# Attention loop over batches written out, row sums inverted on GpSimd instead of VectorE

## The chip, the core and the metric

The kernel runs on one core of a Trainium2 chip. The metric is the time of one execution on the device, in microseconds (us). Engines are named as the profile names them: PE is TensorE (matmuls; PEld its weight loads), DVE is VectorE, ACT is ScalarE, POOL is GpSimd, SP is SyncE, which here issues the DMAs.

## The reference

One transformer block with adaptive layer norm, in float32, on x of shape (4, 512, 128): 4 batches of 512 tokens, width 128. The attention half has 16 heads of width 64 and a relative position bias; the second half is a mixture of 160 experts, top 8 for each token.

```python
mod = (silu(c) @ wmod)                       # shift, scale, gate for both halves
h = layernorm(x) * (1 + ca) + sa
q, k, v = split(h @ qkv_w.T)                 # 16 heads of 64
scores = einsum("bhqd,bhkd->bhqk", q, k) * 64 ** -0.5 + bias
attn = softmax(scores, axis=-1)              # rows of 512
a = einsum("bhqk,bhkd->bhqd", attn, v)
x = x + ga * (a @ o_w.T)
h = layernorm(x) * (1 + cb) + sb
x = x + gb * moe(h)                          # 160 experts, top 8
```

The change touches the softmax (the division by the row sum) and the order of the work around it.

## The kernel before

Each engine has its own instruction stream, written by hand; the streams meet only at semaphores (`wait_ge`, `then_inc`). An engine executes its stream in order, so an instruction that waits holds up everything behind it on that engine.

The attention half takes the batches one after the other. Within a batch the 16 heads go in 8 pairs (`HPAIRS`), `pair(b, n)`. A pair has 8 units (`UNITS`): 2 heads times 4 tiles of 128 query rows. A unit `u` is a 128x512 tile of scores (128 query rows, 512 keys) and passes through these steps:

- PE, `scores` (L409, L411): two matmuls into PSUM bank `BANK_S + g % 2`, so two units at a time.
- DVE, `add_bias` (L976): adds the bias, writes the tile into `prob[:, u, :]` and its negated row maximum into `nmax`. It waits until the tile of the same `u` of the pair before has been transposed.
- ACT, `exponential` (L706): exp in place, with the row sum into `rsum[:, u]`; it counts `s_exp`.
- DVE, `invert_sums` (L993): after every second unit, one reciprocal of the two columns `rsum[:, u:u+2]` into `rinv`; it counts `s_rinv`.
- POOL, `normalise` (L859): multiplies the 128x512 tile by its column of `rinv`; it counts `s_prob`.
- PE, `transpose_probs` (L420): four 128x128 transposes into PSUM; DVE (odd units) or ACT (even units) copies them to `PT` (L204).
- PE, `attend` (L433): 16 matmuls for each pair, `PT` by `v_sb`, into `BANK_O`; DVE, `copy_o` (L999), copies the result to `oT`; PE, `project_out` (L446), adds it to y in `BANK_Y`.

Besides these, every pair projects Q and K of the pair two ahead (`project_qk`, L383; `qk_high` on ACT, `qk_low` on DVE, L959) and V of the next ones (`project_v`, L394), and SP restacks Q and K by DMA (`stack_pair`).

The order is software pipelined by hand: `pair(b, n)` on PE issues scores of pair n, two units at a time, and between them the transposes and `attend` of pairs n, n-1 and n-2. Pairs 8 and 9 of a batch are pairs 0 and 1 of the next one. Pairs (0, 0) and (0, 1) stand alone in the code. Then comes a hardware loop of 3 iterations over the batch, `Fori(0, B - 1)`, with the 8 pairs n = 2 to 9 in its body, on SP, PE, ACT and DVE, and behind it the 6 last pairs of batch 3, written out. POOL has a loop of its own, `Fori(0, B)`, with 64 units in the body. Semaphore counts that depend on the batch are compared with a register inside the loops.

At the end of a batch, in pair n = 9 (`HPAIRS + 1`), DVE gates y (`gate_y`, L1004), PE transposes it (`transpose_y`, L453), and DVE adds it to x (`update_x`, L1019) and takes the statistics of the new x for the second layer norm (`new_statistics`, L1011, four tiles). These two DVE steps are the last ones of the loop's body:

```python
                if n == HPAIRS + 1:
                    update_x(b)
                    new_statistics(b)
```

What waits for `update_x` is `project_out` of the next batch's first pair, issued in its pair 2, since it writes the same PSUM bank. `project_out` waits for `copy_o` too. The expert half after the attention has loops of its own, which the change leaves alone.

Of the kernel before, what the change touches and what calls it, by code (L numbers as in the profile page):

```python
# [24 lines left out]
P = 128  # L25
B, S, D = 4, 512, 128
# [8 lines left out]
HPAIRS = H // 2  # L35
UNITS = 2 * QT
# [19 lines left out]
def adaln_block(nc, x, emb, qkv_t, o_t, router_t, expert_bias, gate_t_in, down_t, gate_shared_t,  # L56
# [4 lines left out]
    G = HPAIRS * UNITS  # L61
# [7 lines left out]
    with ctx:  # L69
        def sb(name, shape, dt=F32):  # L70
            return ctx.enter_context(nc.sbuf_tensor(name, shape, dt))

        def sem(name):
            return ctx.enter_context(nc.semaphore(name))
# [25 lines left out]
        nmax = sb("nmax", [P, UNITS])  # L100
        rsum = sb("rsum", [P, UNITS])
        rinv = sb("rinv", [P, UNITS])
        modT = sb("modT", [P, 6, B])
        gate_t = sb("gate_t", [P, 2, B])
        cT = sb("cT", [P, B])
# [59 lines left out]
        s_s, s_ttr, s_exp, s_t = sem("scores"), sem("biased"), sem("exped"), sem("transposed")  # L165
        s_ca, s_cd = sem("copied_by_act"), sem("copied_by_dve")
        s_v, s_vc, s_pv = sem("v_projected"), sem("v_copied"), sem("pv_done")
        s_rinv, s_prob, s_o = sem("sums_inverted"), sem("normalised"), sem("o_copied")
        s_ymm, s_yg, s_ytr, s_x2 = sem("y_added"), sem("y_gated"), sem("y_transposed"), sem("x_updated")

# [45 lines left out]
        apart = sem("apart")  # L216
# [5 lines left out]
        def _(sp):  # L222
# [32 lines left out]
            def stack_pair(b, n):  # L255

                par = n % 2
                if n >= 2:
                    sp.wait_ge(s_s, b * G + UNITS * (n - 1))
                    sp.sem_inc(apart, 1)  # L260
                projected = b * HPAIRS + (n + 1)
                halves = ((0, slice(0, HD), slice(HD, P)), (1, slice(HD, P), slice(0, HD)))
                sp.wait_ge(s_qkh, projected)
                sp.sem_inc(apart, 1)
                for head, own, _ in halves:
                    sp.dma_start(stack[own, par, head, :, :].bitcast(F32),
                                 qkH[own, :, :].bitcast(F32)).then_inc(s_stack[par], 16)
                sp.wait_ge(s_qkl, projected)
                sp.sem_inc(apart, 1)
                for head, own, other in halves:  # L270
                    sp.dma_start(stack[other, par, head, :, :].bitcast(F32),
                                 qk[own, 0:4:3, :].bitcast(F32)).then_inc(s_stack[par], 16)
                    sp.dma_start(kLow[par][own, head, :].bitcast(F32),
                                 qkL[own, 1, :].bitcast(F32)).then_inc(s_stack[par], 16)
                    sp.dma_start(kLow[par][other, head, :].bitcast(F32),
                                 qkL[own, 1, :].bitcast(F32)).then_inc(s_stack[par], 16)
# [12 lines left out]
            sp.dma_start(wdsT[:, :], down_shared_t).then_inc(ld["small"], 16)  # L289
            sp.dma_start(ebias[:, 0:1], expert_bias[0:P, :]).then_inc(ld["small"], 16)  # L290
            sp.dma_start(ebias[0:E - P, 1:2], expert_bias[P:E, :]).then_inc(ld["small"], 16)
            with sp.Fori(0, B - 1) as b:
                for n in range(2, HPAIRS + 2):
                    if n == HPAIRS - 2:
                        sp.wait_ge(s_v, b * HPAIRS + HPAIRS)
                        sp.sem_inc(apart, 1)
                        sp.dma_start(hcur[:, :, :].bitcast(F32), hT[:, bass.ds(b + 1, 1), :, :].rearrange(
                            "p o l s -> p (o l) s").bitcast(F32)).then_inc(ld["hcur"], 16)
                    stack_pair(b, n + 2)
# [48 lines left out]
        def _(pe):  # L348
# [157 lines left out]
            pair(0, 1)  # L506
            pe.wait_ge(w_split, 6)
            pe.wait_ge(ld["ow"], 16)
            with pe.Fori(0, B - 1) as b:
                for n in range(2, HPAIRS + 2):  # L510
                    pair(b, n)
            for n in range(2, HPAIRS):
# [157 lines left out]
        def _(act):  # L670
# [87 lines left out]
            first_high(1)  # L758
            pair(0, 0)
            pair(0, 1)  # L760
            with act.Fori(0, B - 1) as b:
                for n in range(2, HPAIRS + 2):
                    pair(b, n)
            for n in range(2, HPAIRS):
# [87 lines left out]
        @block.gpsimd  # L852
        def _(pool):
            def normalise(b, n, u):

                if u % 2 == 0:
                    pool.wait_ge(s_rinv, b * (G // 2) + (UNITS * n + u) // 2 + 1)
                    pool.sem_inc(apart, 1)
                nc.gpsimd.tensor_scalar(prob[:, u, :], prob[:, u, :], rinv[:, u:u + 1], None,  # L859
                                        ALU.mult).then_inc(s_prob, 1)  # L860

            with pool.Fori(0, B) as b:
                for n in range(HPAIRS):
                    for u in range(UNITS):
                        normalise(b, n, u)
# [3 lines left out]
        def _(dve):  # L869
# [51 lines left out]
            def first_low(n):  # L921
                b = FIRST_ORDER[n]
                modulated_low(n, hcur if b == 0 else hT[:, b, :, :], h_full[b])
# [33 lines left out]
            def qk_low(b, n):  # L957
                dve.wait_ge(s_qkh, b * HPAIRS + (n + 1))
                nc.vector.tensor_tensor(qkL[:, :, :], ps[:, BANK_PROJ:BANK_PROJ + 2, :],  # L959
                                        qkH[:, :, :].bitcast(F32), ALU.subtract).then_inc(s_qkl, 1)  # L960
# [23 lines left out]
                    dve.wait_ge(s_pv, b * HPAIRS + (n - 1))  # L984
                copy_unit(nc.vector.tensor_copy, n, u).then_inc(s_cd, 1)

            def invert_sums(b, n, u):

                g = UNITS * n + u
                dve.wait_ge(s_exp, b * G + (g + 2))  # L990
                if n >= 1:
                    dve.wait_ge(s_prob, b * G + (g - UNITS + 2))
                nc.vector.reciprocal(rinv[:, u:u + 2], rsum[:, u:u + 2]).then_inc(s_rinv, 1)  # L993

            def copy_o(b, n):
                dve.wait_ge(s_pv, b * HPAIRS + (n + 1))
                if n >= 2:
                    dve.wait_ge(s_ymm, b * HPAIRS + (n - 1))
                nc.vector.tensor_copy(oT[:, n % 2, :], ps[:, BANK_O, :]).then_inc(s_o, 1)  # L999
# [7 lines left out]
            def new_statistics(b):  # L1007

                dve.wait_ge(s_x2, b + (1 + X2_AHEAD))
                for t in range(QT):  # L1010
                    last = nc.vector.bn_stats(  # L1011
                        stats[:, bass.ds(b * QT + t, 1), :].rearrange("p o k -> p (o k)"),
                        x_all[:, bass.ds(b, 1), t * D:(t + 1) * D].rearrange("p o d -> p (o d)"))
                last.then_inc(s_stats, 1)

            def update_x(b):
                dve.wait_ge(s_ytr, b + 1)
                x_b = x_all[:, bass.ds(b, 1), :].rearrange("p o n -> p (o n)")
                nc.vector.tensor_tensor(x_b, x_b, ps[:, BANK_Y, :], ALU.add).then_inc(s_x2, 1)  # L1019

            def pair(b, n, final=False):

                add_bias(b, n, 0)
                add_bias(b, n, 1)
                if n == 0:
                    first_low(1)
                    qk_low(b, 1)
                if n >= 2:
                    copy_o(b, n - 2)
                if n >= 1:  # L1030
                    copy_probs(b, n - 1, 5)
                invert_sums(b, n, 0)

                add_bias(b, n, 2)
                add_bias(b, n, 3)
                if n == 0:
                    modulate(2)
                    modulate(3)
                if n >= 1:
                    copy_probs(b, n - 1, 7)  # L1040
                invert_sums(b, n, 2)

                add_bias(b, n, 4)
                add_bias(b, n, 5)
                if n == HPAIRS + 1:
                    gate_y(b)
                if n == 0:
                    qkv_low(3)
                    qkv_low(4)
                    qkv_low(5)  # L1050
                copy_probs(b, n, 1)
                invert_sums(b, n, 4)

                add_bias(b, n, 6)
                add_bias(b, n, 7)
                if n == 0:
                    first_low(2)
                    first_low(3)
                copy_probs(b, n, 3)
                invert_sums(b, n, 6)  # L1060
                if not (final and n >= HPAIRS - 2):
                    qk_low(b, n + 2)
                if n == HPAIRS + 1:
                    update_x(b)
                    new_statistics(b)

            qk_low(0, 0)
            then(statistics(3))
# [2 lines left out]
            for b in range(1, B):  # L1071
                norm(b, xn)
            modulate(1)
            pair(0, 0)
            pair(0, 1)
            sign_gates()
            with dve.Fori(0, B - 1) as b:
                for n in range(2, HPAIRS + 2):
                    pair(b, n)
            for n in range(2, HPAIRS):  # L1080
# [157 lines left out]
```

## Time and profile before

| | |
|---|---|
| median of 3 runs | 1015.85 us (1013.87 to 1016.39) |
| profiled execution, its own time | 1013.81 us |
| span of the profile | 1012.0 us |
| granted TensorE clock, mean | 0.985 of full speed |
| busy in the span | PE 94%, DVE 76%, ACT 67%, POOL 39% |
| attention half | about 25 to 517 us of the span |
| expert half | the rest |

The span runs from the first to the last instruction of the core; the 1.8 us between span and time lie around it. Busy time is counted for each engine over the whole span, so POOL, which works in the attention half alone, is far busier there than its 39% say. "Idle before" in a row is the time that the engine did nothing just before an instruction, with what released it behind the arrow.

### The profile page before, as it was taken

What the parts mean: (1) busy time and instruction counts of PE and PEld (TensorE: products, weight loads), DVE (VectorE), ACT (ScalarE), POOL (GpSimd) and SP (SyncE); (2) the same over time, 40 slices, a digit from 0 to 9 for tenths busy, and PEclk for the clock granted to TensorE, in tenths of its full rate; (3) what the DMA queues carried; (4) which work ended last, traced back from release to release, by engine and by line L of the source; (5) the groups of instructions that cost most, each with busy time, mean ns of one, the idle gap of its engine ahead of it and who ended that gap; (6) DMA issues with size and microseconds to landing.
All of it is one profiled execution on the core that took longest, in us unless ns stands there. A gap on an engine that the chain in (4) does not pass through costs nothing.

```text
span 1012.0 us, 16804 instructions
## 1 busy us (share of the span) xinstructions
PE 953.2 (94%) x4592; PEld 690.6 (68%) x4592; DVE 769.4 (76%) x1452; ACT 679.4 (67%) x1168; POOL 398.1 (39%) x260
## 2 busy tenths in 40 slices
PE   4889999899998999999969699999999999999997
PEld 2546666566665666666524578888888888888886
DVE  5757667566665666766647589999999999999997
ACT  3556666466665666666626477877777777777775
POOL 0578888688886888888910000000000000000000
PEclk9999999899999999999979899999999999999999
DMA  7885445256444445534200899999999999999991
GB/s 205 258 234 119 97 119 126 63 124 142 113 96 101 96 118 125 125 90 99 66 19 27 204 221 219 223 222 222 223 222 222 221 224 221 223 220 225 220 206 41
DMA packets 71096, 160.39 MB, mean 158 GB/s; under 512 B 10273, under 2 KB 36193, under 8 KB 60945
## 3 DMA queue, kind: packets, MB, share of 16 engines
q1 hardware_dynamic: 71056, 159.97, 70.1%
q8 instruction: 13, 0.21, 0.1%
q14 instruction: 27, 0.21, 0.1%
HBM read 105.60 MB, written 2.42 MB: 107 GB/s over the span
## 4 chain that ended last, share of the span: by engine, by line
PE 84%; DMA 4%; DVE 4%; issue 3%; ACT 2%; SPq 1%; POOL 1%; POOLq 0%; DVEq 0%; ACTq 0%
PE ps L620 40%; PE ps L433 11%; PE ps L420 10%; PE ps L409 5%; PE ps L411 5%; PE ps L383 4%; PE ps L446 3%; PE ps L394 2%; DMA strips<-in_L_ffn_w_down 2%; DMA k_low<-qk 1%; POOL prob L859 1%; DMA comb_rows<-strips 1%; PE ps L538 1%; PE ps L540 0%; DVE qk L959 0%
## 5 line engine op out<-in xcount | busy, mean ns | idle before, releaser
L859 POOL TENSOR_SCALAR prob<-prob,rinv 128x512 f32<-128x512 f32 x256 | 397.9, 1567 | 111.3 <-DVE rinv L993 109.1
L706 ACT ACTIVATE prob<-prob,nmax 128x512 f32<-128x512 f32 x256 | 182.9, 716 | 150.9 <-DVE nmax L976 150.8
L620 PE MATMUL ps<-hT,wT 128*128 128x512 f32 x960 | 244.2, 390 | 0.3 <-DVE wT L1145 0.3
L1164 DVE TENSOR_TENSOR PT<-v_sb,strips 128x1024 f32<-128x1024 f32 x160 | 196.0, 1225 | 41.4 <-ACT v_sb L830 28.3
L830 ACT ACTIVATE v_sb<-ps 128x1024 f32<-128x1024 f32 x160 | 164.5, 1028 | 77.9 <-PE ps L620 77.4
L620 PEld LDWEIGHTS ps<-hT,wT 128*128 128x128 f32 x960 | 180.8, 189 | 39.0 <-ACT strips L805 1.1
L620 PE MATMUL ps<-stack,wT 128*128 128x512 f32 x640 | 198.1, 391 | 9.2 <-DVE wT L1151 9.2
L204 DVE COPY PT<-ps 128x512 f32<-128x512 f32 x128 | 88.4, 691 | 141.2 <-PE ps L420 138.7
L1151 DVE TENSOR_TENSOR wT<-PT,stack 128x1024 fp32r<-128x1024 f32 x160 | 195.0, 1219 | 0.0
L976 DVE CUSTOM_DVE_ANT_0 prob<-ps,strips 128x512 f32<-128x512 f32 x256 | 165.0, 681 | 11.5 <-issue 8.0
L822 ACT CAST stack<-PT 128x1024 fp32r<-128x1024 f32 x160 | 166.6, 1041 | 8.8 <-DVE PT L1164 8.8
L420 PEld LDWEIGHTS ps<-ident,prob 128*128 128x128 f32 x1024 | 114.7, 141 | 76.8 <-issue 39.1
L620 PEld LDWEIGHTS ps<-stack,wT 128*128 128x128 f32 x640 | 120.3, 189 | 35.7 <-DVE wT L1151 10.9
L420 PE MATMUL ps<-ident,prob 128*128 128x128 f32 x1024 | 137.5, 277 | 2.9 <-ACT PT L204 1.4
L409 PE MATMUL ps<-stack 128*128 128x512 f32 x256 | 114.3, 447 | 15.7 <-DVE nmax L976 9.9
L433 PE MATMUL ps<-PT,v_sb 128*64 128x512 f32 x512 | 124.5, 608 | 2.6 <-ACT PT L204 1.4
L620 PE MATMUL ps<-wT 128*128 128x512 f32 x320 | 99.0, 391 | 0.0
L204 ACT COPY PT<-ps 128x512 f32<-128x512 f32 x128 | 73.9, 578 | 20.8 <-PE ps L420 20.8
L433 PEld LDWEIGHTS ps<-PT,v_sb 128*64 128x64 f32 x512 | 31.8, 137 | 63.1 <-issue 50.8
L620 PEld LDWEIGHTS ps<-wT 128*128 128x128 f32 x320 | 60.4, 189 | 12.6
L409 PEld LDWEIGHTS ps<-stack 128*128 128x128 f32 x256 | 49.4, 193 | 23.9 <-DVE nmax L976 11.8
L383 PE MATMUL ps<-hcur,wT 128*128 128x512 f32 x192 | 52.2, 409 | 3.5 <-DVE hcur L918 3.5
(105 smaller groups left out, 731.1 us busy)
## 6 DMA issues: line engine op xcount, KB each, us to landing
strips<-comb_rows SPq DMA_DIRECT2D x158, 512.0 KB, 10.9
stack<-qk SPq DMA_DIRECT2D x128, 256.0 KB, 3.8
k_low<-qk SPq DMA_DIRECT2D x64, 128.0 KB, 3.9
hT<-qk SPq DMA_DIRECT2D x64, 128.0 KB, 3.8
strips<-bias_rows SPq DMA_DIRECT2D x3, 1792.0 KB, 13.9
strips<-in_L_ffn_w_gate SPq DMA_DIRECT2D x80, 64.0 KB, 9.8
strips<-in_L_ffn_w_down SPq DMA_DIRECT2D x80, 64.0 KB, 11.0
strips<-bias_rows SPq DMA_DIRECT2D x2, 896.0 KB, 5.4
```

The lines of the kernel that those rows point to most:

```text
L204: return copy(dst[:, :, qt * P:(qt + 1) * P], ps[:, BANK_T + u % 2, :].rearrange("p (k s) -> p k s", s=P))
L409: nc.tensor.matmul(ps[:, BANK_S + g % 2, :], stack[:, par, head, 0, qt * P:(qt + 1) * P], stack[:, par, head, 1, :], start=True, stop=False)
L420: last = nc.tensor.transpose(ps[:, BANK_T + u % 2, kb * P:(kb + 1) * P], prob[:, u, kb * P:(kb + 1) * P], ident[:, :])
L433: last = nc.tensor.matmul(ps[head * HD:(head + 1) * HD, BANK_O, :], v_sb[:, (n // 2) % 2, kb, (n % 2) * P + head * HD:(n % 2) * P + (head ...
L620: last = nc.tensor.matmul(ps[:, bank + c, :], weights(a), rows(m, c), start=start and k == 0, stop=stop and k == 2, skip_group_check=True)
L706: nc.scalar.activation(prob[:, u, :], prob[:, u, :], ACT.Exp, bias=nmax[:, u:u + 1], scale=-1.0, accum_out=rsum[:, u:u + 1]).then_inc(s_ex ...
L822: nc.scalar.copy(h_high[:, k % 4, :], weighted[:, k % 4, :]).then_inc(s_hh, 1)
L830: nc.scalar.activation(silu[:, k % 2, :], ps[:, BANK_G + 2 * half:BANK_G + 2 * half + 2, :].rearrange("p c s -> p (c s)"), ACT.Silu).then_ ...
L859: nc.gpsimd.tensor_scalar(prob[:, u, :], prob[:, u, :], rinv[:, u:u + 1], None, ALU.mult).then_inc(s_prob, 1)
L976: nc.vector.tensor_tensor_reduce(out=prob[:, u, :], in0=ps[:, BANK_S + u % 2, :], in1=backwards, scale=-1.0, scalar=3.0e38, op0=ALU.add, o ...
L1151: nc.vector.tensor_tensor(h_low[:, k % 4, :], weighted[:, k % 4, :], h_high[:, k % 4, :].bitcast(F32), ALU.subtract).then_inc(s_hl, 1)
L1164: nc.vector.tensor_tensor(weighted[:, k % 4, :], silu[:, k % 2, :], cb[:, r, half * HALF:(half + 1) * HALF], ALU.mult).then_inc(s_mul, 1)
```

## The change

1. The loops over the batch are ordinary Python loops, on SP, PE, ACT, DVE and POOL: their 3 (POOL: 4) iterations are written out as straight code, with constant semaphore counts.
2. `invert_sums` is gone from DVE. POOL does it in `normalise`, with a `tensor_tensor` power of -1 on the same two columns (the exponents in a new 128x2 tile `minus_one`, filled once), and waits for its own result before the multiplication.
3. `update_x` and `new_statistics` of a batch move on DVE from the end of its pair 9 to the next pair (pair 2 of the next batch), behind `add_bias` of units 0 and 1 and ahead of `copy_o`.

```diff
+        minus_one = sb("minus_one", [P, 2])
...
+        s_exponents = sem("exponents_set")
...
-            with sp.Fori(0, B - 1) as b:
+            for b in range(B - 1):
                 for n in range(2, HPAIRS + 2):
...
-            with pe.Fori(0, B - 1) as b:
+            for b in range(B - 1):
...
-            with act.Fori(0, B - 1) as b:
+            for b in range(B - 1):
...
+                g = UNITS * n + u
                 if u % 2 == 0:
-                    pool.wait_ge(s_rinv, b * (G // 2) + (UNITS * n + u) // 2 + 1)
-                    pool.sem_inc(apart, 1)
+                    pool.wait_ge(s_exp, b * G + (g + 2))
+                    nc.gpsimd.tensor_tensor(rinv[:, u:u + 2], rsum[:, u:u + 2], minus_one[:, :], ALU.pow).then_inc(s_rinv, 1)
+                    pool.wait_ge(s_rinv, b * (G // 2) + g // 2 + 1)
                 nc.gpsimd.tensor_scalar(prob[:, u, :], prob[:, u, :], rinv[:, u:u + 1], None,
                                         ALU.mult).then_inc(s_prob, 1)
...
-            with pool.Fori(0, B) as b:
+            nc.gpsimd.memset(minus_one[:, :], -1.0).then_inc(s_exponents, 1)
+            pool.wait_ge(s_exponents, 1)
+            for b in range(B):
...
-            def invert_sums(b, n, u):
-
-                g = UNITS * n + u
-                dve.wait_ge(s_exp, b * G + (g + 2))
-                if n >= 1:
-                    dve.wait_ge(s_prob, b * G + (g - UNITS + 2))
-                nc.vector.reciprocal(rinv[:, u:u + 2], rsum[:, u:u + 2]).then_inc(s_rinv, 1)
...
                 if n == 0:
                     first_low(1)
                     qk_low(b, 1)
+                if n == 2 and b >= 1:
+                    update_x(b - 1)
+                    new_statistics(b - 1)
                 if n >= 2:
                     copy_o(b, n - 2)
                 if n >= 1:
                     copy_probs(b, n - 1, 5)
-                invert_sums(b, n, 0)
...
-                if n == HPAIRS + 1:
-                    update_x(b)
-                    new_statistics(b)
...
-            with dve.Fori(0, B - 1) as b:
+            for b in range(B - 1):
                 for n in range(2, HPAIRS + 2):
                     pair(b, n)
```

The other three calls of `invert_sums` in `pair` (units 2, 4 and 6) go as well.

## Rows read from the trace of the kernel before

**Rows 1.** The page, busy shares and POOL's line over 40 equal slices.

```profile
PE 953.2 (94%) x4592; PEld 690.6 (68%) x4592; DVE 769.4 (76%) x1452; ACT 679.4 (67%) x1168; POOL 398.1 (39%) x260
...
POOL 0578888688886888888910000000000000000000
```

**Rows 2.** Busy time by stretch: us, PE, PEld, DVE, ACT, POOL, PEclk, DMA, GB/s.

```profile
180.00:202.00 22.00, 17.36 (x82) 11.19 (x83) 11.80 (x32) 9.57 (x22) 12.77 (x9) 0.84 0.31 73
201.50:301.00 99.50, 99.50 (x551) 65.78 (x550) 68.02 (x184) 66.71 (x155) 86.99 (x57) 1.00 0.50 116
...
437.46:508.00 70.54, 70.52 (x387) 44.54 (x386) 48.57 (x131) 45.87 (x109) 63.46 (x42) 1.00 0.42 96
```

**Rows 3.** Waits from 208.7 to 293.7 us: total us, times, longest.

```profile
POOL prob L859 <- DVE rinv L993: 10.0, 18, 0.8
```

**Rows 4.** The chain that ended last: start us, us, what; some of the attends, transpose of y, one wait.

```profile
158.29 1.87 PE ps L433 x8
...
172.49 1.87 PE ps L433 x8
...
176.32 0.44 PE ps L453 x4
...
182.56 3.65 issue
...
194.50 1.94 PE ps L433 x8
...
293.73 1.87 PE ps L433 x8
...
314.88 1.94 PE ps L433 x8
...
414.35 1.87 PE ps L433 x8
...
430.40 1.94 PE ps L433 x8
...
444.64 1.87 PE ps L433 x8
```

**Rows 5.** Timeline where the loop jumps back: start us, us, what, [idle before].

```profile
180.85 0.68 DVE L1019 TENSOR_TENSOR x_all<-x_all,ps 128x512 f32 x1
...
181.70 1.00 DVE L1011 BATCH_NORM_STATS2 stats<-x_all  x4 [0.17 <-DVE x_all L1019]
...
186.57 0.69 DVE L976 CUSTOM_DVE_ANT_0 prob<-ps,strips 128x512 f32<-128x512 f32 x1 [3.87 <-issue]
...
187.32 0.80 PE L409 MATMUL ps<-stack 128*128 128x512 f32 x1 [4.50 <-DVE nmax L976]
```

**Rows 6.** Timeline of an undisturbed pair, units 0 and 1.

```profile
260.37 0.69 DVE L999 COPY oT<-ps 128x512 f32<-128x512 f32 x1
...
261.21 0.19 ACT L706 ACTIVATION_READ_ACCUMULATOR prob<-prob,nmax 128x1 f32 x1
...
261.76 0.16 DVE L993 RECIPROCAL rinv<-rsum 128x2 f32<-128x2 f32 x1
...
262.12 3.10 POOL L859 TENSOR_SCALAR prob<-prob,rinv 128x512 f32<-128x512 f32 x2 [0.70 <-DVE rinv L993]
...
262.58 1.02 PE L446 MATMUL ps<-oT,woT 128*128 128x512 f32 x2
```

**Rows 7.** Groups and lines: durations (mean ns, or min/median/max) on POOL and DVE.

```profile
L859 POOL TENSOR_SCALAR prob<-prob,rinv 128x512 f32<-128x512 f32 x256 | 397.9, 1567 | 111.3 <-DVE rinv L993 109.1
L1226 POOL MEMSET const-float32-0.0<- 128x1 f32 x1 | 0.1, 99 | 0.2 <-issue 0.2
...
L993 DVE RECIPROCAL rinv<-rsum x128: 148/155/167, 36.3 to 505.3; 128x2 f32<-128x2 f32 x128
...
L976 DVE CUSTOM_DVE_ANT_0 prob<-ps,strips 128x512 f32<-128x512 f32 x256 | 165.0, 681 | 11.5 <-issue 8.0
```

**Rows 8.** Timeline, POOL at the end of the attention half.

```profile
491.12 18.51 POOL L859 TENSOR_SCALAR prob<-prob,rinv 128x512 f32<-128x512 f32 x12 [0.71 <-DVE rinv L993]
```

More of the change, by code:

```diff
@@ L1040, in pair @@
                     copy_probs(b, n - 1, 7)
-                invert_sums(b, n, 2)
                 add_bias(b, n, 4)
@@ L1051, in pair @@
                 copy_probs(b, n, 1)
-                invert_sums(b, n, 4)
                 add_bias(b, n, 6)
@@ L1059, in pair @@
                 copy_probs(b, n, 3)
-                invert_sums(b, n, 6)
                 if not (final and n >= HPAIRS - 2):
                     qk_low(b, n + 2)
-                if n == HPAIRS + 1:
-                    update_x(b)
-                    new_statistics(b)
             qk_low(0, 0)
```

## The prediction

> **What bounds the kernel now.** I began with the page. PE is busy for 94% of the span; POOL's 39% is an average over a half where it works and one where it has nothing to do, and in the slices of the attention half it stands at 8 tenths [rows 1]. So two engines matter for the change: PE, which probably sets the pace, and POOL, to which work is added. The busy time by stretch shows that first guess to be right: from 201.5 to 301 us PE is busy for 99.50 of 99.50 us, POOL for 86.99, or 87%, and DVE for 68% [rows 2]. In an undisturbed stretch nothing but PE's own work sets the time; a faster DVE or POOL gains nothing there.
>
> The chain that ended last gives the beat. An `attend` block comes back every pair: 172.49 - 158.29 = 14.20 us [rows 4]. POOL's share of a pair is 8 tiles. It ran 12 of them in 18.51 us where it never waited, and 3.10 us is a usual time for two [rows 6, 8], so 1.56 us each and 12.5 us a pair; 14.20 - 12.5 = 1.7 us are free. The waits agree: over 85 us, six pairs, POOL waited 10.0 us for the reciprocals, 1.67 us a pair [rows 3].
>
> Then I looked for where PE doesn't keep this beat. The same block around the batch boundaries, each step holding one pair: 194.50 - 172.49 = 22.01, 314.88 - 293.73 = 21.15, and 430.40 - 414.35 = 16.05 us [rows 4]. Against 14.20 these are 7.8, 6.95 and 1.85 us too much, 16.6 us in all. The first two boundaries are those where the loop jumps back, the third falls out of the loop. The timeline says what the jump does: DVE has finished the statistics at 182.7 us and then stands for 3.87 us waiting for nothing but its own next instruction, PE idles 4.50 us for the bias tile that comes after it [rows 5], and the granted clock of that stretch falls to 0.84, between the levels of 2.4 and 1.2 GHz, after that idle time [rows 2].
>
> **The change, part by part.**
>
> *Loops written out.* The two jumps go. What shows their price is the third boundary, which has the same work and no jump: 7.8 + 6.95 - 2 x 1.85 = 11.05 us. Straight code does not run slower: the last batch is written out already and keeps its pair in 444.64 - 430.40 = 14.24 us [rows 4], with PE busy for 70.52 of 70.54 us [rows 2]. The jumps of PE, ACT, SP and POOL lie under DVE's, and they go too. Gain 11.05 us; the bounds are 0 (if fetching the code stalls elsewhere) and 15 (the whole excess of both).
>
> The Trainium skill, Runtime: NRT & Kernel Launch, section Instruction fetch mechanics, says that a jump out of the small window of loaded code costs a fetch, while straight code is prefetched. That explains the 3.65 us of "issue" [rows 4], and by it too the jumps would be the whole price.
>
> *`update_x` and `new_statistics` moved.* At the third boundary they hold DVE for 0.68 + 0.17 + 1.00 us [rows 5] in front of `add_bias`, and PE pays 1.85 us. Of these, 0.44 us is PE's own transposing of y [rows 4], which stays. In the new place two tiles of bias go first and PE can go on with the scores; late is now `copy_o`. In an undisturbed pair it starts at 260.37 and ends at 261.06, and `project_out`, which needs it, starts at 262.58 [rows 6]: 1.52 us of cover against 1.85 + 0.1 us of delay, so PE waits about 0.5 us. New price of a boundary: 0.44 + 0.5, say 0.95 us instead of 1.85, for three boundaries a gain of 2.7 us. Bounds: 0, and 4.2 if the delay is hidden altogether. If POOL has no slack left, the same delay (the exponentials of units 2 and 3 come 1.9 us later) falls on it as well.
>
> *Reciprocal off DVE.* 128 reciprocals of 155 ns [rows 7], 0.6 us a pair, on an engine that is not the bound: nothing by itself. What hides them is PE's full beat. Without them POOL no longer waits behind DVE's queue: the row sum of unit 1 is out at 261.40, the reciprocal begins at 261.76 and POOL starts 0.70 us after its last tile [rows 6]. That wait is room for the new work, and it is the 1.7 us a pair counted above.
>
> *The power on POOL.* Four a pair, 128 in all; each costs POOL its duration d and a wait s for its own result, since the multiplication behind it cannot be handed over before. For s a row is near: DVE waits 0.17 us between an instruction and its dependent one [rows 5]. For d there is none: the trace has no power and no small two-input instruction on POOL. From below: a POOL memset of 128x1 takes 0.10 us [rows 7]. From above: if the whole duration of a 128x512 multiplication were fixed, 1.56 us. Between them, DVE does the same 128x2 shape in 0.155 us, and POOL is 1567/681 = 2.3 times as slow as DVE on a 128x512 tile [rows 7]: 0.36 us. The power itself is unknown work on only 2 columns. I take the middle of 0.10 and 0.36, d = 0.23, as the operation is nearest to these small rows, and so d + s = 0.40 us. Four make 1.6 us, and POOL has 1.7 us. So it just fits: undisturbed pairs keep 14.20 us. The whole argument hangs here, and the room left is 0.02 us in each power. Where it doesn't fit, POOL sets the beat and each 0.01 us above 0.42 costs 4 x 0.01 x 30 pairs = 1.2 us.
>
> The Trainium skill, GPSIMD Engine Reference, section Performance versus the Vector engine, speaks against this part: ordinary elementwise work is about 1.96 times slower there. By an estimate from that page and DVE's 155 ns, d would be 0.30 and the sum further down would read -5 instead of -12 us; no run here shows a two-input instruction on POOL.
>
> *The end of the attention half.* In the last two pairs PE has less to do, and POOL runs its last 12 tiles without a pause from 491.12 us [rows 8]; what follows waits for its last tile. There the powers are not hidden: six of them at 0.40, of which the first begins 0.7 us earlier than the tile did. That is 6 x 0.40 - 0.7 = +1.7 us. At the start, POOL's first tiles also follow each other closely, but PE then waits for a DMA, which hides it.
>
> *Sum.* -11.05 - 2.7 + 1.7 = -12.05 us against the profiled execution's own 1013.81: 1001.8 us. That execution was 2.0 us below the median of the runs; I put half of that on top for a median: **1002.7 us**.
>
> **Rivals.**
>
> - *POOL becomes the bound.* This one ends on the other side. For it: 87% busy already, and four dependent small instructions more a pair. Against: their size, if the small rows are a guide. With x = d + s the change is -13.75 + (6x - 0.7) + 120 (x - 0.42) us. It is zero at x = 0.515, that is d = 0.345 us: from there on the gain is eaten. At d = 0.6 (x = 0.77) the sum is 31.6 us, 1045 us; at the upper bound d = 1.56 it is +154 us, 1168 us. Chance 0.26 for d above 0.35 by enough to be seen.
> - *It fits only partly*: x between 0.42 and 0.515, and the time between 1002 and 1014 us. For it: the ratio row gives just the upper end. Chance 0.17, most of it still faster than the bound below.
> - *Writing out brings nothing*: the stall at the batch boundary is not the jump but code that has to be loaded, and the far longer streams stall somewhere else. Against it speaks the third boundary, without a stall, and the last batch. Time: 1013.8 - 2.7 + 1.7 = 1012.8 us. Chance 0.07.
>
> **How the numbers follow.** The forecast itself (x up to 0.42) has 0.50. A measurement of this kernel can tell about 0.3%, 3 us, from no change. Faster: 0.50 + 0.13 from the partial case + 0.02 from the third rival = 0.65. Same: 0.03 + 0.05 = 0.08. Slower: 0.26 + 0.01 = 0.27. Both signs hold a good part, so the range is wide: its low end, 996 us, is the sum with all three boundaries free of excess (-16.6 and a little off the end), its high end, 1045 us, is POOL as the bound with d = 0.6; beyond it I leave 0.14, below it 0.04. The likeliest case alone lies between 998 and 1006 us.
>
> **What the profile after should show.** The 3.65 us of "issue" on the chain and the 4.50 us idle of PE are gone at both boundaries, and the granted clock stays at 1.00 there. The `attend` steps over the three boundaries are about 15.1 us. A new POOL row, 128 powers of 128x2, some 0.2 us each, followed by about 0.17 us of waiting for itself. POOL is busy for over 90% of an undisturbed pair, which still takes 14.2 us with PE fully busy. If instead the `attend` steps are all longer than 14.2 and PE waits for POOL's `prob`, the size of the power was wrong, and the excess of a pair divided by four tells by how much. What would make the prediction wrong is that one number, far more than all others.

## The result, and the profile after

| | median | runs | ratio to before, 95% interval |
|---|---|---|---|
| before | 1014.89 us | 1013.87 to 1016.39 | |
| after | 1043.38 us | 1042.78 to 1044.88 | 1.0282 [1.0262, 1.0301] |

The changed kernel is 28.5 us, 2.8%, slower. The forecast was 1002.7 us, faster: the sign was wrong. The time lies at the upper edge of the range, where the first rival stood, with 0.26: POOL becomes the bound. The kernel before ran again beside each group of experiments, and every ratio is to those runs: their medians were 1014.89 us here, 1014.66 us beside e1 to e4, and 1015.95 us beside e5 to e8.

The page of the changed kernel: busy shares, PE's and POOL's line over the slices, the chain by engine and by line, and the two POOL groups.

```profile
PE 966.4 (93%) x4592; PEld 684.4 (66%) x4592; DVE 764.3 (73%) x1324; ACT 679.8 (65%) x1168; POOL 487.9 (47%) x389
...
PE   4789999999999999999977699999999999999997
...
POOL 0689999999999999999960000000000000000000
...
PE 44%; POOL 44%; DMA 4%; DVE 2%; issue 2%; SPq 2%; ACT 1%; POOLq 0%; ACTq 0%; DVEq 0%
PE ps L622 39%; POOL prob L863 36%; POOL rinv L861 8%; DMA strips<-in_L_ffn_w_down 2%; DMA k_low<-qk 2%; SPq L315 1%; DMA comb_rows<-strips 1%; PE ps L540 1%; PE ps L385 0%; PE ps L435 0%; PE ps L542 0%; PE ps L555 0%; ACT qk L704 0%; PE ps L593 0%; PE ps L355 0%
...
L863 POOL TENSOR_SCALAR prob<-prob,rinv 128x512 f32<-128x512 f32 x256 | 399.8, 1573 | 12.6
...
L861 POOL TENSOR_TENSOR rinv<-rsum,minus_one 128x2 f32<-128x2 f32 x128 | 92.0, 719 | 35.8 <-ACT prob L708 35.8
```

POOL stands at 9 tenths where it stood at 8 [rows 1]. On the chain it has 44% of the span, all of it in the attention half, where the chain ran over PE before. The power is a row of 128 instructions of 719 ns. POOL's idle time is 35.8 us, nearly all before its first power, against 111.3 us before [rows 7].

Busy time in 77.9 us, five pairs of POOL's new beat (columns as in [rows 2]), and POOL's timeline there:

```profile
208.30:286.20 77.90, 73.87 (x391) 46.37 (x390) 47.58 (x111) 47.33 (x111) 75.93 (x61) 1.00 0.46 109
```

```profile
201.84 0.72 POOL L861 TENSOR_TENSOR rinv<-rsum,minus_one 128x2 f32<-128x2 f32 x1
202.66 3.11 POOL L863 TENSOR_SCALAR prob<-prob,rinv 128x512 f32<-128x512 f32 x2
205.73 0.72 POOL L861 TENSOR_TENSOR rinv<-rsum,minus_one 128x2 f32<-128x2 f32 x1
206.55 3.11 POOL L863 TENSOR_SCALAR prob<-prob,rinv 128x512 f32<-128x512 f32 x2
```

Two tiles start every 206.55 - 202.66 = 3.89 us: 3.11 of tiles, 0.68 of power (it takes 0.72 but begins 0.04 before the tile ahead has ended) and 0.10 until the tile behind it starts. Four of these are 15.58 us a pair (so one is 3.895 us, more exactly), where PE set 14.20 before. PE is now the one that waits, busy for 73.87 of 77.90 us (before, 99.50 of 99.50 [rows 2]).

The boundary of the batches, where 7.8 us were lost before, from PE's timeline:

```profile
172.28 1.94 PE L435 MATMUL ps<-PT,v_sb 128*64 128x512 f32 x8
...
178.56 0.66 PE L422 MATMUL ps<-ident,prob 128*128 128x128 f32 x4 [0.32 <-POOL prob L863]
...
187.87 1.51 PE L435 MATMUL ps<-PT,v_sb 128*64 128x512 f32 x6
```

The step is 187.87 - 172.28 = 15.59 us, the 15.58 us of any pair, so the stall of the jump is gone. Nothing else of the boundary is left in the step either: whatever PE or DVE loses there hides behind POOL.

### The profile page after: what moved, and what is told of

Same layout as the page of the kernel before. It is cut to its first block, busy times and chain, and to the rows that moved or that the text cites. A ratio compares the mean times of both kernels' runs of the same rounds, so it can differ in the third digit from the quotient of the medians.

```text
span 1041.4 us, 15577 instructions
## 1 busy us (share of the span) xinstructions
PE 966.4 (93%) x4592; PEld 684.4 (66%) x4592; DVE 764.3 (73%) x1324; ACT 679.8 (65%) x1168; POOL 487.9 (47%) x389
## 4 chain that ended last, share of the span: by engine, by line
PE 44%; POOL 44%; DMA 4%; DVE 2%; issue 2%; SPq 2%; ACT 1%; POOLq 0%; ACTq 0%; DVEq 0%
PE ps L622 39%; POOL prob L863 36%; POOL rinv L861 8%; DMA strips<-in_L_ffn_w_down 2%; DMA k_low<-qk 2%; SPq L315 1%; DMA comb_rows<-strips 1%; PE ps L540 1%; PE ps L385 0%; PE ps L435 0%; PE ps L542 0%; PE ps L555 0%; ACT qk L704 0%; PE ps L593 0%; PE ps L355 0%
## 5 line engine op out<-in xcount | busy, mean ns | idle before, releaser
L422 PEld LDWEIGHTS ps<-ident,prob 128*128 128x128 f32 x1024 | 112.5, 141 | 121.9 <-issue 57.3
L422 PE MATMUL ps<-ident,prob 128*128 128x128 f32 x1024 | 154.3, 283 | 28.9 <-POOL prob L863 28.2
L435 PE MATMUL ps<-PT,v_sb 128*64 128x512 f32 x512 | 127.4, 620 | 1.9 <-ACT PT L206 1.1
L861 POOL TENSOR_TENSOR rinv<-rsum,minus_one 128x2 f32<-128x2 f32 x128 | 92.0, 719 | 35.8 <-ACT prob L708 35.8
```

The source lines that it names most:

```text
L422: last = nc.tensor.transpose(ps[:, BANK_T + u % 2, kb * P:(kb + 1) * P], prob[:, u, kb * P:(kb + 1) * P], ident[:, :])
L861: nc.gpsimd.tensor_tensor(rinv[:, u:u + 2], rsum[:, u:u + 2], minus_one[:, :], ALU.pow).then_inc(s_rinv, 1)
```

## The experiments

The theory after the result: the power costs POOL 0.72 us and not 0.23; POOL sets the beat; the rest of the change is a gain. Eight kernels test this against its rivals.

### e1 and e2: without the power

e1 is the kernel before with the loops written out; the `sem_inc` behind each POOL wait, which stood only in the loop, goes with them. e2 is the changed kernel with `invert_sums` back on DVE, so it differs from e1 by the moved update of x:

```diff
-            with dve.Fori(0, B - 1) as b:
+            for b in range(B - 1):
```

That was e1 against before, on all five engines alike. e2 against after, where the call on DVE stands for units 2, 4 and 6 too:

```diff
-                    nc.gpsimd.tensor_tensor(rinv[:, u:u + 2], rsum[:, u:u + 2], minus_one[:, :], ALU.pow).then_inc(s_rinv, 1)
...
+                invert_sums(b, n, 0)
```

Expected of e1:

> The kernel before with the batch loops written out on all engines and nothing else. Theory A (the power's 0.72 us on POOL is the whole loss, writing out is a gain of its own): the jumps' price goes, 1014.9 - 11 = about 1004 us, the two PE waits of 4.5 us are gone and DVE's 3.87 us of issue too. Theory B (the long straight streams themselves are loaded more slowly, and that is part of the loss): 1015 us or above, with stalls named issue or by engine queues spread over the attention half.

Expected of e2:

> The changed kernel with the reciprocals back on DVE: loops written out and the update of x moved, no power on POOL. Theory A: 1004 - 2.7 = about 1001 us, with some 15.1 us for the attend steps across the three boundaries. Rival: the move only shifts the delay from the bias tiles to the copy of o and gains nothing, then it equals the written-out kernel, about 1004 us. Theory B: no better than 1015 us.

Measured: e1 1001.67 us, ratio 0.9870 [0.9854, 0.9887]; e2 1000.33 us, 0.9865 [0.9849, 0.9881]. Writing out is a gain, and a rival in which straight code stalls falls with it. DVE's idle time named issue before its bias tiles is 0.2 us in all in e1, against 8.0 us before [rows 7], and the granted clock at the first boundary (180 to 195 us) is 1.00, where it was 0.84 [rows 2]. The chain of e1 across two boundaries:

```profile
172.45 1.87 PE ps L435 x8
188.03 1.94 PE ps L435 x8
...
287.27 1.87 PE ps L435 x8
302.85 1.94 PE ps L435 x8
```

The steps are 15.58 us, the third one (417.66 - 402.08) as well, against 22.01, 21.15 and 16.05 before [rows 4]: 12.5 us less in sum, against a gain of 13.0 us measured. It is more than the 11.05 expected, since the third boundary, which had no stall, became 0.47 us shorter too, and each of the others by as much again. DVE's timeline at the third boundary before, and at the first one in e1:

```profile
422.71 0.68 DVE L1019 TENSOR_TENSOR x_all<-x_all,ps 128x512 f32 x1
...
424.65 0.69 DVE L976 CUSTOM_DVE_ANT_0 prob<-ps,strips 128x512 f32<-128x512 f32 x1
```

```profile
180.81 0.67 DVE L1020 TENSOR_TENSOR x_all<-x_all,ps 128x512 f32<-128x512 f32 x1
...
181.52 0.87 DVE L1012 BATCH_NORM_STATS2 stats<-x_all 128x6 f32<-128x128 f32 x4
...
182.31 0.67 DVE L977 CUSTOM_DVE_ANT_0 prob<-ps,strips 128x512 f32<-128x512 f32 x1
```

From the update of x to the next bias tile DVE takes 1.94 us in the loop and 1.50 us in straight code (the same at its other two boundaries): it waits 0.04 us for its own result instead of 0.17, and the four statistics take 0.87 us instead of 1.00 [rows 5].

In e2 the step is still 15.58 us, not the 15.1 expected: the move gained nothing at the boundary, as the rival had it. That e2's time nevertheless came out at theory A's 1001 us is luck. The profiled executions of e1 and e2 differ by 3.0 us already at 172.45 and 169.49 us, the last `attend` on the chain ahead of the first boundary, up to which the move changes nothing, and the intervals of the two ratios overlap. e2's timeline there:

```profile
179.06 0.68 DVE L1020 TENSOR_TENSOR x_all<-x_all,ps 128x512 f32<-128x512 f32 x1
...
179.78 0.88 DVE L1012 BATCH_NORM_STATS2 stats<-x_all 128x6 f32<-128x128 f32 x4
...
180.57 0.68 DVE L1000 COPY oT<-ps 128x512 f32<-128x512 f32 x1
...
181.30 1.13 PE L448 MATMUL ps<-oT,woT 128*128 128x512 f32 x2
...
181.83 0.67 DVE L977 CUSTOM_DVE_ANT_0 prob<-ps,strips 128x512 f32<-128x512 f32 x1
...
182.54 0.72 ACT L708 ACTIVATE prob<-prob,nmax 128x512 f32<-128x512 f32 x1 [1.98 <-DVE nmax L977]
...
184.44 0.58 ACT L206 COPY PT<-ps 128x512 f32<-128x512 f32 x1
...
185.07 1.51 PE L435 MATMUL ps<-PT,v_sb 128*64 128x512 f32 x6 [0.85 <-ACT PT L206]
```

`project_out` (L448) starts in its turn, 0.05 us after `copy_o` (L1000) ends, so the cover over `copy_o` held better than forecast. What is late is the bias of units 2 and 3 (L977), then ACT, which waits 1.98 us for it, and then ACT's copy to `PT`, queued behind two exponentials and the copy of V: `attend` waits 0.85 us for it.

### e3: the power alone

The kernel before with loops and order kept, and the power on POOL in place of `invert_sums`:

```diff
                 if u % 2 == 0:
-                    pool.wait_ge(s_rinv, b * (G // 2) + (UNITS * n + u) // 2 + 1)
+                    pool.wait_ge(s_exp, b * G + (g + 2))
                     pool.sem_inc(apart, 1)
+                    nc.gpsimd.tensor_tensor(rinv[:, u:u + 2], rsum[:, u:u + 2], minus_one[:, :], ALU.pow).then_inc(s_rinv, 1)
+                    pool.wait_ge(s_rinv, b * (G // 2) + g // 2 + 1)
+                    pool.sem_inc(apart, 1)
```

> The kernel before, loops kept and update of x in its old place, with the reciprocals replaced by the power on POOL. Theory A (POOL sets the beat of 3.9 us for two units, 15.6 us a pair): slower than the changed kernel's 1043.4, since the jumps still stop DVE and POOL runs dry there: POOL idled 6.2 us at each jump before, of which its work ahead hides part, so 1047 to 1054 us. Theory B (half of the loss is from the straight code): below 1035 us.

Measured: 1062.42 us, 1.0471 [1.0453, 1.0488]. The direction is theory A's, the size is above its 1047 to 1054. So on top of the power, the written-out loops and the move together are worth 19.0 us (e3 against after), more than the 14.5 us without it (e2 against before). POOL's timeline says why:

```profile
185.27 3.11 POOL L865 TENSOR_SCALAR prob<-prob,rinv 128x512 f32<-128x512 f32 x2 [0.21 <-POOL rinv L862]
...
189.28 3.11 POOL L865 TENSOR_SCALAR prob<-prob,rinv 128x512 f32<-128x512 f32 x2 [0.21 <-POOL rinv L862]
...
199.16 0.72 POOL L862 TENSOR_TENSOR rinv<-rsum,minus_one 128x2 f32<-128x2 f32 x1 [2.77 <-ACT prob L708]
```

At the jump POOL runs dry for 2.77 us, and for 2.74 us at the second one: 5.5 us. And its beat is 4.01 us instead of 3.89, since it stands 0.21 us between the power and the tile, against 0.10 in the changed kernel: 128 x 0.11 = 14 us, which the expectation did not have. Together 19.5 us. e3 also has the update of x in its old place. POOL does not wait at the third boundary, which has that update and no jump, so the update alone does not run it dry; what share it has in the 5.5 us, no run tells. In the loop the wait is against a register and followed by a semaphore increment; which of the two costs the 0.11 us, no run tells apart.

### e4: a list of prices on POOL

e2 with scratch instructions, each waiting for the one before, in POOL's idle time at the start:

```python
            nc.gpsimd.tensor_tensor(pc[:, 0:2], pa[:, 0:2], pb[:, 0:2], ALU.pow).then_inc(s_pa, 1)
            pool.wait_ge(s_pa, 3)
            ...
```

> The kernel of e2 with extra instructions at the head of POOL's stream, where it has 36 us to spare, on scratch tiles: powers of 2, 4, 16 and 64 columns, two-input products of 2 and 64 columns, a one-input product of 2 and 256 columns, a copy of 2 columns, each twice. Theory fixed (every small two-input instruction on POOL costs about 0.7 us): the product of 2 columns takes about 0.7 us as the power does, and 4 columns cost no more than 2. Theory per element (the power is computed column by column at a high price): the product of 2 columns takes 0.1 to 0.2 us, and the power grows by about 0.3 us a column, so 1.3 us for 4 and 5 us for 16. The whole time may be some us above e2 if the list takes longer than the spare time.

Measured: 1001.37 us (one run), and the timeline of POOL's first 36 us; L869 to L883 are powers, L885 to L891 products of two tiles, L893 and L901 products with a column of scalars. The list ended at 36.8 us, and POOL's first tile started 3.2 us later than in e2 (36.86 against 33.67 us); the time lies within e2's range all the same (999.17 to 1002.34 us).

```profile
1.21 0.72 POOL L869 TENSOR_TENSOR pc<-pa,pb 128x2 f32<-128x2 f32 x1
2.01 0.70 POOL L871 TENSOR_TENSOR pc<-pa,pb 128x2 f32<-128x2 f32 x1
...
2.79 1.01 POOL L873 TENSOR_TENSOR pc<-pa,pb 128x4 f32<-128x4 f32 x1
...
4.96 2.90 POOL L877 TENSOR_TENSOR pc<-pa,pb 128x16 f32<-128x16 f32 x1
...
10.91 10.54 POOL L881 TENSOR_TENSOR pc<-pa,pb 128x64 f32<-128x64 f32 x1
...
32.16 0.19 POOL L885 TENSOR_TENSOR pc<-pa,pb 128x2 f32<-128x2 f32 x1
...
32.71 0.32 POOL L889 TENSOR_TENSOR pc<-pa,pb 128x64 f32<-128x64 f32 x1
...
33.53 0.30 POOL L893 TENSOR_SCALAR pc<-pa 128x2 f32<-128x2 f32 x1
...
34.81 0.93 POOL L901 TENSOR_SCALAR pc<-pa 128x256 f32<-128x256 f32 x1
```

A power costs (10.54 - 2.90)/48 = 0.16 us a column, as it does from 4 to 16 columns, and some 0.4 us that don't depend on the width. A product of the same shape costs 0.19 us, and 0.002 us a column. Neither theory is right alone: of the 0.72 us, about 0.2 us is what the product of the same shape costs, 0.3 us are the two columns, and the other 0.2 us is a fixed part of the power. The price by the column is there, but half of the 0.3 us expected. The second power is as dear as the first (0.70 us), so no cost of a first use shows.

### e5, e6 and e7: the beat, moved from three sides

All three are the changed kernel with one thing else. e5 puts a product in place of the power. e6 keeps the power and makes the tiles narrower. e7 puts a product in its place that is nearly as long as the power. The waits stay. What they leave out is a right result: e5 scales the rows by a wrong factor, e6 leaves the last 96 columns of each tile unscaled, e7 scales every tile by a constant. In this order, e5, e6 and e7:

```diff
-                    nc.gpsimd.tensor_tensor(rinv[:, u:u + 2], rsum[:, u:u + 2], minus_one[:, :], ALU.pow).then_inc(s_rinv, 1)
+                    nc.gpsimd.tensor_tensor(rinv[:, u:u + 2], rsum[:, u:u + 2], minus_one[:, :], ALU.mult).then_inc(s_rinv, 1)
```

```diff
-                nc.gpsimd.tensor_scalar(prob[:, u, :], prob[:, u, :], rinv[:, u:u + 1], None,
+                nc.gpsimd.tensor_scalar(prob[:, u, 0:416], prob[:, u, 0:416], rinv[:, u:u + 1], None,
```

```diff
-                    nc.gpsimd.tensor_tensor(rinv[:, u:u + 2], rsum[:, u:u + 2], minus_one[:, :], ALU.pow).then_inc(s_rinv, 1)
+                    nc.gpsimd.tensor_tensor(pc[:, :], pa[:, :], pb[:, :], ALU.mult).then_inc(s_rinv, 1)
```

> The changed kernel with the power replaced by a two-input product on the same 128x2 tiles, so the rows are scaled by the wrong factor; all waits stay. The list of prices gave 0.195 us for it against 0.70 to 0.72. Theory size (only d matters, POOL has 0.42 us for each power and its wait): 0.195 + 0.10 fits, POOL needs 13.6 us a pair, PE sets the beat of 14.2 again, and the time is that of e2, 1000 to 1002 us. Rival (the dependent wait and the wait for the exponential on POOL itself cost it the beat, whatever the operation): well above 1010 us, with POOL idle before the products.

> The changed kernel with the power kept, but POOL normalises only 416 of the 512 columns of each tile; the other 96 stay unnormalised. Theory size: 96 columns are 0.24 us by the list of prices (2.5 ns a column), 1.9 us a pair, so POOL needs 15.58 - 1.9 = 13.7 us a pair, less than PE's 14.2, and the whole loss goes though all 128 powers are there: 1000 to 1003 us. Rival (the power's latency in the chain from the exponential to the transpose is what PE pays): it stays above 1030 us.

> The changed kernel with the power replaced by a two-input product of 128x176 scratch columns, whose result nothing uses; the tiles are scaled by a constant. By the list of prices it takes 0.195 + 174 x 0.0021 = 0.56 us, and with the wait 0.66 us. Theory size: the time falls by 128 for each us less than the power's 0.785: 1043.4 - 128 x 0.125 = about 1027 us, 15.1 us a pair. Rival (a threshold or anything special to the power, such as its code being loaded each time): e5's time, about 1001 us, since it is a plain product too.

| | two tiles every | POOL a pair | time | ratio, 95% interval |
|---|---|---|---|---|
| after | 3.89 us | 15.58 us | 1043.38 us | 1.0282 [1.0262, 1.0301] |
| e7, product of 176 columns | 3.73 us | 14.9 us | 1022.6 us | 1.0062 [1.0037, 1.0087] |
| e6, tiles of 416 columns | at least 3.42 us | 13.7 us | 1003.19 us | 0.9874 [0.9835, 0.9914] |
| e5, product of 2 columns | at least 3.36 us | 13.4 us | 1002.94 us | 0.9870 [0.9832, 0.9908] |
| e2, no inversion on POOL | PE's beat | 12.5 us | 1000.33 us | 0.9865 [0.9849, 0.9881] |

The second column is from start to start of tiles on POOL's timeline, where POOL does not wait; e7's is half of two beats. Rows of that kind, of e5, e6 and e7:

```profile
202.32 3.10 POOL L863 TENSOR_SCALAR prob<-prob,rinv 128x512 f32<-128x512 f32 x2
...
205.68 3.11 POOL L863 TENSOR_SCALAR prob<-prob,rinv 128x512 f32<-128x512 f32 x2
...
212.83 0.20 POOL L861 TENSOR_TENSOR rinv<-rsum,minus_one 128x2 f32<-128x2 f32 x1 [0.67 <-ACT prob L708]
```

```profile
202.05 2.64 POOL L863 TENSOR_SCALAR prob<-prob,rinv 128x416 f32<-128x416 f32 x2
...
205.47 2.64 POOL L863 TENSOR_SCALAR prob<-prob,rinv 128x416 f32<-128x416 f32 x2
```

```profile
203.60 3.10 POOL L865 TENSOR_SCALAR prob<-prob,rinv 128x512 f32<-128x512 f32 x2
...
211.06 3.10 POOL L865 TENSOR_SCALAR prob<-prob,rinv 128x512 f32<-128x512 f32 x2
```

Busy time in the same 77.9 us, of e5:

```profile
208.30:286.20 77.90, 77.90 (x432) 51.28 (x431) 53.51 (x122) 52.32 (x124) 71.70 (x67) 1.00 0.53 124
```

and of e6 and e7:

```profile
208.30:286.20 77.90, 77.90 (x431) 51.28 (x431) 53.38 (x123) 52.35 (x123) 73.08 (x66) 1.00 0.54 126
```

```profile
208.30:286.20 77.90, 76.17 (x408) 48.99 (x407) 49.18 (x115) 50.06 (x116) 75.84 (x64) 1.00 0.45 109
```

With the product PE is busy all the time again and POOL waits for ACT, though every wait of the new order is there: the duration sets the loss, not the waits. e6 has all 128 powers at full price and PE is busy all the time too: it is not the power's latency in the chain of a unit. e7 is a plain product, and slower than the kernel before: the loss belongs to the length and not to the power. From e7 to the changed kernel the beat grows by 3.895 - 3.73 = 0.165 us, 128 times that is 21 us, and the time grows by 20.8 us (22 us by the ratios). The same slope reaches e2's 1000 us at 3.56 us, about a quarter of PE's 14.20. So a pair takes as long as the slower of the two engines needs for it.

Three misses are small. e5 and e6 lie 1 us or less above the time expected, and some 2.7 us above e2's, with intervals that overlap; of this, 0.7 and 1.2 us are a longer end of the attention half (from one and the same `attend` to the last one 495.64 - 443.39 = 52.25 us in e2, 499.45 - 446.50 = 52.95 in e5, 498.65 - 445.23 = 53.42 in e6). e7 came out 4 us below its 1027: its beat was 0.62 us above the tiles' 3.11, where the expectation had added 0.56 and 0.10 without their overlap of 0.04.

### e8: the statistics later

e2 with `new_statistics` behind the bias of units 2 and 3, where DVE waits for PE anyway:

```diff
                 if n == 2 and b >= 1:
                     update_x(b - 1)
-                    new_statistics(b - 1)
...
+                if n == 2 and b >= 1:
+                    new_statistics(b - 1)
                 if n >= 1:
                     copy_probs(b, n - 1, 7)
```

> e2 with the statistics of the new x taken out of their place behind update_x and put behind the bias of units 2 and 3, where DVE waits for PE; update_x stays where the change puts it. In e2 the step across a boundary is still 15.58 us, as with the loops written out alone: the bias of units 2 and 3 comes 1.5 us late, ACT exponentiates them late, and its copies behind them reach the attend 0.85 us late. Theory: with 0.9 us less on DVE in front, that wait is gone, the steps are 14.7 to 14.8 us and the time 2.4 us below e2's, about 998 us. Rival: what is left is PE's own work and the clock, then the steps stay 15.58 us and the time about 1000 us.

Measured: 999.57 us, 0.9842 [0.9812, 0.9872]. The chain across the first boundary and the second:

```profile
171.52 1.87 PE ps L435 x8
...
186.21 1.94 PE ps L435 x8
...
285.68 1.87 PE ps L435 x8
...
300.36 1.94 PE ps L435 x8
```

The steps are 14.69 and 14.68 us, 0.9 us shorter than e2's at each of three boundaries; what is left over 14.20 is about PE's 0.44 us of transposing y. The chain shows the 2.7 us. The median is only 0.8 us below e2's and above the 998 us expected, and the intervals overlap, so the timed runs do not separate e8 from e2; e8's profiled execution was 2.0 us behind e2's before the first boundary. This kernel has the lowest median here, 1.6% under the kernel before.

## Why the prediction was wrong, by its steps

- *What bounds the kernel*: right. PE's beat of 14.20 us and POOL's 1.7 us of room a pair came out nearly as read. e5, e6 and e7 show the threshold: up to 3.42 us for two tiles PE stays busy all the time, at 3.73 us it does not. A quarter of 14.20 less the 3.11 us of two tiles leaves 0.44 us for a power and its wait, where the prediction had 0.42 (18.51 us for 12 tiles are 1.54 us each, not the 1.56 it went on with).
- *Loops written out*, 11.05 us expected: 12.5 us by the steps, 13.0 us by the time (e1). Right for the stall, a little small: DVE's update of x also runs some 0.4 us shorter outside the loop, at all three boundaries. The Trainium skill, Runtime: NRT & Kernel Launch, section Instruction fetch mechanics, has straight code prefetched and a far jump fetched; the trace agrees: DVE stood 3.87 us at the jump, and in e1 0.2 us in all before the same tiles.
- *Update of x moved*, 2.7 us expected: nothing at the boundary (e2 against e1). Here the mechanism was wrong. I followed the delay to `copy_o` and `project_out`, whose cover held, and did not follow it through the bias of units 2 and 3 to ACT's queue. Moving the statistics behind that bias brings the gain, 0.9 us a boundary (e8).
- *Reciprocal off DVE*: worth nothing by itself, as forecast; e5, without it, is no faster than e2.
- *The end of the attention half*: right as a formula. 6x - 0.7 gives 0.8 us for e5's x of 3.36 - 3.11 = 0.25 us, and 0.7 us was measured.
- *The power on POOL* is the step that failed, and by its size only: d = 0.23 us was forecast from the middle of 0.10 and 0.36 us, and 0.72 us measured. With its wait the forecast had 0.40 us, just inside the room of 0.42; it was 0.785, so POOL's pair took 15.58 us instead of fitting into 14.20, and the sign turned. The error was in the choice of rows. The memset and the multiplication are other operations, and the reciprocal ran on another engine; none of the rows is of a power on POOL. My 0.23 would have been nearly right for the product of the same shape, 0.19 us (e4). I kept the 1.56 us of a full tile as the upper bound but gave the room above 0.35 us only 0.26, though nothing in the trace spoke for it being empty. By the Trainium skill's ratio for elementwise work (GPSIMD Engine Reference, section Performance versus the Vector engine), 1.96, d would by estimate have been 0.30 us; it is a ratio for an addition, and the power measured 0.72 us, the product 0.19 us (e4).
- *The wait for its own result*, 0.17 us: 0.10 measured, 0.21 in a loop (e3). The row that it was taken from stood in a loop as well; DVE's own wait there shrank to 0.04 us in straight code (e1).
- *The rival's formula*, with the measured x = 3.895 - 3.11 = 0.785 us, gives -13.75 + 4.0 + 43.8 = +34 us, measured +28.5. The 120 (x - 0.42) should have been 30 x (15.58 - 14.20) = 41.4, and the 2.9 us that it left standing at the boundaries hide behind POOL; with both mended it gives +28.8 us. The formula was also worked out slightly wrong where its examples stand: d = 0.6 gives +32.2 us and not 31.6, the upper bound +153 and not +154, and d = 0.30 a sum of -5.6 and not -5. The high end of the range, 1045 us, rests on the first of these; the measured time is inside with either.

So the loss of 28.5 us is 43 us for the power (after against e2) less 14.5 us for the rest (e2 against before).

## What to carry to other kernels

For an engine that is 87% busy beside a full one the budget can be read closely, here 0.42 us against the 0.44 us found; what decides is whether the price of the new instruction is known as well as the budget. Where the trace has no row for it, put it first of all in that engine's idle time, as e4 did at no cost that its one run shows, before the rest is built on it. And follow a delay through every queue behind the delayed instruction, not only to the first instruction that waits for it.

## What the hardware showed beyond that

- A power of 128x2 on POOL takes 0.70 to 0.72 us, and each further column 0.16 us, so 10.54 us for 64, where a product of 64 columns takes 0.32 us.
- A one-input product with a column of scalars on POOL is dearer at 2 columns (0.30 us) than a product of two tiles (0.19 us).
- The wait of a POOL instruction for the one ahead cost 0.10 us in straight code and 0.21 us in the hardware loop, 14 us over the run (e3); DVE's wait for the update of x went from 0.17 to 0.04 us (e1).
